# Four attention and feed-forward layers on one core: the weights' spreading merged with the pick of queries, and loads of the last layer issued during its normalisation

## The reference, cut to what matters

```python
scores = q @ k.T * scale
sparsity = scores.max(axis=-1) - scores.mean(axis=-1)
_, top_idx = jax.lax.top_k(sparsity, U)          # U = 153 queries of each head
...
out = zeros_like(q).at[bi, hi, top_idx].set(softmax(scores_sel) @ v)
return out @ Wo + bo
...
combine = zeros((T, E)).at[arange(T)[:, None], tidx].add(tw)
routed = sum over e of combine[:, e] * (relu2(xf @ up_w[e]) @ down_w[e])
```

```python
out = softmax((q @ k.T + causal + bias) / dh) @ v
s = out @ Wo + bo
h = silu(xn @ dequant(w_gate).T) * (xn @ dequant(w_up).T)
g = silu(h @ dequant(w_down).T)
```

## Time and profile before

| | us |
|---|---|
| median of 3 runs | 4108.3 |
| lowest and highest | 4107.21 and 4111.95 |
| the profiled execution's own time | 4112.44 |
| its span, from the first to the last instruction | 4110.6 |

### The profile page before, as it was taken

How to read it: one execution, slowest core, us unless ns; L and a number is a source line. 1 busy time by engine, 2 the same in 40 slices (tenths; PEclk the granted TensorE clock), 3 DMA queues, 4 the chain that set the end, 5 groups by cost and what they waited for, 6 DMA issues and landing times. The chain is left out here.

```text
span 4110.6 us, 86910 instructions
## 1 busy us (share of the span) xinstructions
PE 3561.5 (87%) x28212; PEld 2164.2 (53%) x28212; DVE 2452.7 (60%) x5699; ACT 2020.7 (49%) x3970; POOL 1263.6 (31%) x1810
## 2 busy tenths in 40 slices
PE   5799999959996788894999986788985599999997
PEld 2344444437773222222677753268973366666664
DVE  5667677631113688885677776427645566666664
ACT  6466666633335477772333334233243465656562
POOL 0111111100001011110677762506474244444440
PEclk9799999979997799996999987787687799999998
DMA  4322222100001311110666631030005233333330
GB/s 128 79 55 57 54 58 54 48 11 6 11 6 49 76 46 43 42 30 13 176 163 157 157 83 61 34 101 3 3 17 72 80 116 114 117 113 117 114 104 27
DMA packets 198051, 287.18 MB, mean 70 GB/s; under 512 B 40922, under 2 KB 155296, under 8 KB 197460
## 3 DMA queue, kind: packets, MB, share of 16 engines
q1 hardware_dynamic: 193688, 275.28, 24.1%
q0 software_dynamic: 4096, 8.40, 1.5%
HBM read 232.38 MB, written 35.84 MB: 65 GB/s over the span
## 5 line engine op out<-in xcount | busy, mean ns | idle before, releaser
L709 ACT ACTIVATE att_E<-att_pX,att_gs 128x512 f32<-128x512 f32 (+3 forms) x1024 | 723.5, 740 | 423.5 <-PE att_pX L643 177.0
L742 DVE TENSOR_REDUCE att_mx<-att_pS 128x1 f32<-128x512 f32 (+4 forms) x960 | 732.4, 787 | 204.9 <-PE att_pS L617 173.0
L1855 POOL TENSOR_TENSOR att_E<-att_E,att_rz 128x128 f32<-128x128 f32 (+3 forms) x512 | 358.1, 720 | 435.3 <-DVE att_rz L2063 435.3
L637 PE MATMUL att_pX<-arr_qs,arr_ks 75*128 75x512 bf16 (+4 forms) x1536 | 427.3, 334 | 28.0 <-ACT att_E L709 12.8
L612 PE MATMUL att_pS<-arr_ks,arr_qs 72*128 72x512 bf16 (+4 forms) x1536 | 410.5, 339 | 44.1 <-DVE att_pO L732 12.6
L1583 POOL TENSOR_TENSOR pairs_h<-pairs_m,pairs_r 128x512 f32<-128x512 f32 x272 | 346.2, 1273 | 245.8 <-DVE pairs_m L1646 127.2
L574 POOL CAST att_mp<-att_m 16x128 bf16<-16x128 f32 x288 | 81.2, 282 | 935.2 <-DVE att_m L753 910.0
L1607 PEld LDWEIGHTS pairs_po<-pairs_a,pairs_h 128*128 128x128 f32 x2176 | 286.1, 192 | 130.2 <-issue 128.4
L654 PE MATMUL att_pO<-att_E,att_vs 128*9 128x512 f32 (+3 forms) x3072 | 328.9, 500 | 1.3 <-ACT att_E L709 1.3
L1628 ACT ACTIVATE pairs_r<-pairs_ph 128x512 f32<-128x512 f32 x272 | 162.6, 598 | 326.9 <-PE pairs_ph L1599 326.9
L1994 ACT ACTIVATE att_E<-att_S,att_nm 128x128 f32<-128x128 f32 (+3 forms) x512 | 282.0, 556 | 38.4 <-DVE att_nm L2057 38.4
(11 more groups left out here) (411 smaller groups left out, 6527.9 us busy)
## 6 DMA issues: line engine op xcount, KB each, us to landing
pairs_c<-weights SPq DMA_DIRECT2D x272, 256.0 KB, 3.9
att_bias<-in_bias_dram SPq DMA_DIRECT2D x64, 896.0 KB, 4.5
parts<-proj_part SPq DMA_DIRECT2D x144, 128.0 KB, 2.3
att_xb<-xnT SPq DMA_DIRECT2D x64, 256.0 KB, 2.7
arr_qs<-parts SPq DMA_DIRECT2D x192, 64.0 KB
arr_ks<-parts SPq DMA_DIRECT2D x192, 64.0 KB
att_w<-in_w3a_dram SPq DMA_DIRECT2D x64, 192.0 KB, 2.4
arr_qs<-parts SPq DMA_DIRECT2D x96, 96.0 KB
```

The source lines that it names most:

```text
L637: ins = nc.tensor.matmul(dst[:, n], ks[:, g % NB, x, kt * P:(kt + 1) * P], qs[:, g % NB, x, q0(kt):], start=(apart or n == 0), stop=not ca ...
L709: nc.scalar.activation(E[:, kt % 2, WIDE * xp:WIDE * (xp + 1), :w], places(c)[0], ACT.Exp, scale=gs[:, g % 2, gain_of:gain_of + 1]).then_i ...
L742: V.reduce_max(dst, src, AX.X).then_inc(s_mx, 1)
L1855: nc.gpsimd.tensor_tensor(E[:, k, :width(j)], E[:, k, :width(j)], rz[:, u, k:k + 1].broadcast_to([P, width(j)]), ALU.mult).then_inc(s_n, 1)
```

## The change

The spreading becomes part of the pick's body block: PE's transposes of `comb` stand behind its transposes of the sparsity, ACT's copies and SP's writes come along, and the two fills move from DVE to GpSimd. On SP the write of the ones is now the last of the nine and not the first. `s_out` belongs to a phase `spread` around it, which is cleared when it is left.

```diff
 def pick_phase(nc, R, name, negmax, total, count, mask, comb, NE, cT, s_out):
...
+            @block.gpsimd
+            def _(pool):
+                nc.gpsimd.memset(wt[NE:, :], 1.0).then_inc(s_one, 1)
+                pool.drain()
+                nc.gpsimd.memset(R.f[:, :, :], 0.0)
+            @block.sync
+            def _(sp):
+                for n in range(B):
+                    sp.wait_ge(s_wt, n + 1)
+                    sp.dma_start(cT[:NE, n * T:(n + 1) * T], wt[:NE, n * T:(n + 1) * T]).then_inc(s_out, 16)
+                sp.wait_ge(s_one, 1)
+                sp.dma_start(cT[NE:, :], wt[NE:, :]).then_inc(s_out, 16)
+                sp.wait_ge(s_out, 16 * (B + 1))
+            @block.scalar
+            def _(act):
+                for n in range(B):
+                    act.wait_ge(s_turn, n + 1)
+                    nc.scalar.activation(wt[:NE, n * T:(n + 1) * T], pW[:NE, n % 2], ACT.Copy).then_inc(s_wt, 1)
...
                 ins.then_inc(s_t, 1)
+                for n in range(B):
+                    if n >= 2:
+                        pe.wait_ge(s_wt, n - 1)
+                    for q in range(QT):
+                        ins = nc.tensor.transpose(pW[:NE, n % 2, q * P:(q + 1) * P], comb[:, n * QT + q], R.ident[:, :])
+                    ins.then_inc(s_turn, 1)
                 pe.wait_ge(s_mk, 1)
...
-        spread_phase(nc, R, "spread", comb, 64, cT)
-        pick_phase(nc, R, "pick", negmax, total, int(0.6 * 256), mask)
+        with phase(nc, "spread") as p:
+            pick_phase(nc, R, "pick", negmax, total, int(0.6 * 256), mask, comb, 64, cT, p.sem("out"))
```

```diff
 def layer3(nc, R, t, before):
-    norm_phase(nc, R, "norm3", before, lambda sp: None)
-    layer3_attention(nc, R, t)
-    layer3_gate(nc, R, t)
+    with phase(nc, "pre3") as p:
+        bo, wo = p.sb("bo", [P, QT * D]), p.sb("wo", [P, 8, P])
+        wi = p.sb("wi", [P, 3, 3, P], I32)
+        s_c, s_in = p.sem("c"), p.sem("in")
+
+        def ahead(sp):
+            sp.dma_start(bo[:, :], t["bo3"]).then_inc(s_c, 16)
+            for a in range(8):
+                sp.dma_start(wo[:, a], t["wo3"][a]).then_inc(s_c, 16)
+            sp.dma_start(wi[:, :, :, :].rearrange("p k u f -> p (k u f)"), t["w3"]).then_inc(s_in, 16)
+
+        norm_phase(nc, R, "norm3", before, ahead)
+        layer3_attention(nc, R, t, bo, wo, s_c)
+        layer3_gate(nc, R, wi, s_in)
```

More of the change, by code:

```diff
@@ L1313, in layer0_gate, with pick_phase @@
         experts_phase(nc, R, "ex0", 6, t["w1_0"], t["b1_0"], t["w2_0"], wts)
-def pick_phase(nc, R, name, negmax, total, count, mask):
+def pick_phase(nc, R, name, negmax, total, count, mask, comb, NE, cT, s_out):
     with phase(nc, name) as p:
@@ L1330, in pick_phase @@
         s_sp, s_t, s_mk, s_m = p.sem("sp"), p.sem("t"), p.sem("mk"), p.sem("m")
+        wt = p.sb("wt", [cT.shape[0], B * T])
+        pW = p.ps("pW", [P, 2, T])
+        s_one, s_turn, s_wt = p.sem("one"), p.sem("turn"), p.sem("wt")
         scale = DH ** -0.5
         with nc.Block() as block:
+            @block.gpsimd
[16 more added lines that the diff above has]
+                    nc.scalar.activation(wt[:NE, n * T:(n + 1) * T], pW[:NE, n % 2], ACT.Copy).then_inc(s_wt, 1)
             @block.vector
@@ L1480, in routing @@
         yield step
[L1483 to L1520, removed]
 def pairs_phase(nc, R, name, NPAIR, w1, w2, cT):
@@ L1663, in _, with layer3_gate @@
                 run_bodies(dve, NBODY, body)
-def layer3_gate(nc, R, t):
+def layer3_gate(nc, R, wi, s_in):
     U = 3
     with phase(nc, "glu") as p:
-        wi = p.sb("wi", [P, 3, U, P], I32)
         w = p.sb("w", [P, 3, U, P])
@@ L1676, in layer3_gate @@
         po = p.ps("po", [P, 2, T])
-        s_in, s_w, s_up, s_g, s_h, s_d, s_o, s_f = (p.sem(k) for k in ("in", "w", "up", "g", "h", "d", "o", "f"))
+        s_w, s_up, s_g, s_h, s_d, s_o, s_f = (p.sem(k) for k in ("w", "up", "g", "h", "d", "o", "f"))
         NBODY = B // 2
@@ L1680, in layer3_gate @@
         with nc.Block() as block:
-            @block.sync
-            def _(sp):
-                sp.dma_start(wi[:, :, :, :].rearrange("p k u f -> p (k u f)"), t["w3"]).then_inc(s_in, 16)
             @block.scalar
@@ L1758, in _, with layer3_attention @@
                 run_bodies(dve, NBODY, body)
-def layer3_attention(nc, R, t):
+def layer3_attention(nc, R, t, bo, wo, s_c):
     PAIRS, DW = 8, 64
@@ L1778, in layer3_attention @@
         w = p.sb("w", [P, 2, 3, P])
-        wo = p.sb("wo", [P, PAIRS, P])
         xb = p.sb("xb", [P, 2, T])
@@ L1790, in layer3_attention @@
         oT = p.sb("oT", [P, T])
-        bo = p.sb("bo", [P, QT * D])
         pA = p.ps("pA", [P, T])
@@ L1795, in layer3_attention @@
         pO = p.ps("pO", [P, T])
-        s_c = p.sem("c")
         s_z = p.sem("z")
@@ L1826, in _ @@
             def _(sp):
-                sp.dma_start(bo[:, :], t["bo3"]).then_inc(s_c, 16)
-                for a in range(PAIRS):
-                    sp.dma_start(wo[:, a], t["wo3"][a]).then_inc(s_c, 16)
                 def body(i, first, last):
```

## The result

The changed kernel takes 4087.98 us, the median of 5 runs (4087.44 to 4091.93). The kernel before, run more often by then, has a median of 4110.95 (5 runs). The ratio is 0.9947 with a 95% interval of 0.9937 to 0.9958, so 17 to 26 us less: faster by over 0.2%. The forecast was 4087.3, and 21.0 us less.

A forecast was written before the change was run, and what follows sets the result against it. PE is busy 87% on average, but the touched places were bound by SP's writes (13.3 us), then DVE (38.3), and by loads at layer 3's openings. 13.35 - 0.4 + 4.56 + 3.9 - 0.4 = 21.0 us less: 4087.3, range 4081.5 to 4095.

The forecast's parts named there:

- Spreading into pick: Layer 1, attention's end to pick: DVE's pick list starts where the spreading's block started, a gain of 13.35 us.
- Cover: In the merged pick: SP through some 16 us after the start, GpSimd's fills 8.4 to 20.4, hidden beside DVE's 38.3.
- DVE's list beside it: In the merged pick: DVE alone is the path for 38.3 us, next phase's first DVE instruction about 38.7 later.
- Rival (b): In the pick: GpSimd's fills hold up DVE, 4.2 to 16.1 us of the gain go, 4091.5 to 4103.4; chance 0.09.
- Loads: Ten loads issued free in layer 3's normalisation; xb last at the attention's opening, gain 4.56; gated unit's opening, 3.9 us.
- Clearing blocks: Behind the pick and behind the gated unit: one semaphore-clearing block each on the path, costing 0.4 us each.
- Clock: Granted clock at layer 3's openings: counted 0; gated unit 1.5 us gained or up to 2 lost, attention plus or minus 1.5.
- Rival (c): Last attention stays at the low clock, rising 60 us later: 30 us lost, 4117; chance 0.02.
- The spread of runs: Whole kernel's time: 2 us allowed for what medians differ by, added to the forecast's bounds, giving 4081 to 4094.7.

The follow-up runs named there:

- the later kernel: Changed kernel with half a fill of R.f, then nine fills on GpSimd in place of one; pick to next phase 41.25 us instead of 38.6.

## Why the prediction was right

- **Spreading into pick, 13.35**: measured 14.48 - 1.19 = 13.29. Taking the block's start from the fills' spacing and not from the row was decisive for 0.9 us of it, and the run with the fills back on DVE shows why.
- **Cover**: SP was put at 16 us; its last wait was over about 13 us after the start, and GpSimd's fills after 7.2. Here a size was off: the estimate for a fill, 4.2 to 8.0 us by eight times the short ones, missed the 3.64 from the first fill's start to the second's. The half fill of the later kernel took 1.81 us and a whole one 3.52, so 2048 elements more cost 1.71; by that, about 0.1 of the 0.525 us for 512 does not grow with the length.
- **DVE's list beside it**: 38.3 was to become 38.7 with the clearing block; it is 38.6 to 38.8, by two things that were not foreseen and cancel, which is luck. PE's transposes of the sparsity ran at the high clock (1.00), so that DVE waited 0.75 for them and not 1.21 (in the kernel without `xb` the clock was 0.50 there, DVE waited 1.21, and the stretch took 39.06); and DVE has a gap of 0.44 us late in the rounds, at which it waited for nothing that the profile shows. It is there in each profile of the merged pick, at 0.31 where the fills are on DVE. Its cause was not tried.
- **Rival (b)**: it did not come, but the reason given against it was too wide. The pick's list does hold an instruction that waits for a fill, the mask's. What saves it is the order: it starts 28 us behind the fills' end.
- **Loads**: the copy starts with the block and xb is last, as said; 8.11 to 3.35 and, in the gated unit, DVE's wait from 4.81 to 0.90, so 4.76 and 3.91 for the 4.56 and 3.9. That their issue costs the normalisation nothing holds: it takes 31.84 to 32.12 us in the three profiles without them and 31.76 to 32.37 in the ten with them.
- **Clearing blocks, 0.4 each**: 0.38 and 0.44, the second among 0.3 us that come and go there.
- **Clock, 0 with bounds**: it did not stay up in the gated unit; it fell about 4004 and rose before 4008, and the unit's stretch lies between the two of before. In the attention it rose 13 us after the first projection, 12 before. Rival (c) had nothing for it.
- **The spread of runs** was sized too small: the 2 us allowed for what medians differ by came from three runs within 5 us, and 23 runs later lay within 22. The median before moved by 2.65 from 3 runs to 5. The forecast's nearness to the median, 0.7 us, is partly luck: from the later median before, 4110.95, the same 21.0 would have given 4090.0, 2 us above what was measured. The nearness of the sums, 21.0 and 21.1, is not, but for the two things that cancel in DVE's list.

## What to carry to other kernels

Where phases stand end to end, look for two of which one is bound by transfers and the other by one engine: merged, the shorter one costs nothing, and the price is read from the first instruction of each block. When an engine's idle list takes over fills, look for instructions of the other engine that wait for a fill and have the fills over before them; here it was the one that stood out by its speed, 0.43 us for 512 elements where `max` and `match_replace` took 0.68 to 0.70. And a gain of half a per cent is better shown by summing the touched stretches over several profiles than by the medians, as untouched phases moved by 8.4 us here in one kernel.

## What was not expected of the hardware

A fill on DVE takes 4.33 us from others while its row shows 3.47, with the missing 0.9 ahead of the row, while on GpSimd the row of 3.51 nearly fills the 3.64 to the next start. A mask instruction of 0.43 us took 3.08 beside a GpSimd fill that had 2.8 us to go. The gap ahead of the final phase differs by 0.3 us between kernels that are alike there. And one phase of 64 matmuls, with the same instructions, took 59.5 and 49.7 us in two executions of one kernel, at a granted clock of 0.64 and 0.67: why was not tried.
